# A decoder kernel on one core: the context first, row sums on 128 columns, late loads in two parts, and GpSimd in the rounding of the last causal steps

## The reference

```python
x = x + recurrent(ln(x), Wq1, Wq2, Wk1, Wk2, Wv, Wo, norm_w)  # q*scan(v), divided by its root mean square, @ Wo
x = x + experts(ln(x), token_ids, ctx, ctx, ctx)              # 4 experts, chosen by token id; ctx is the weight
x = x + ternary_linear(ln(x), weight, bias)
x = x + causal_attention(ln(x), w_project, w_out)             # 16 heads of 16
x = x + gqa_fp8(ln(x), cond=ctx, wq, wqx, wk, wv, w_kv_x, wproj)
#   xq = fp8(bf16(clip(ln_out / in_scale, -448, 448)))  for the four kinds q, qx, k, v
x = x + moe(ln(x), w_router, w_gate, w_up, w_down, shared...)
```

## Time and profile before

| | us |
|---|---|
| three timed runs | 924.49, 930.89, 932.22 |
| their median | 930.89 |
| the profiled execution | 927.09 |
| its span, first to last instruction | 924.3 |
| TensorE busy in the span | 857.9 (93%) |
| VectorE busy | 702.9 (76%) |
| ScalarE busy | 563.3 (61%) |
| GpSimd busy | 133.7 (14%) |
| mean granted clock of TensorE | 0.982 of full speed |

### The profile page before, as it was taken

The page is one execution under the profiler, slowest core; times in us unless marked ns, Lnnn a source line. Parts: engine busy times, 40 slices in busy tenths (PEclk is TensorE's granted clock), DMA queues, the critical chain, the costliest instruction groups (busy, mean ns, idle before and its releaser), DMA issues.

```text
span 924.3 us, 14815 instructions
## 1 busy us (share of the span) xinstructions
PE 857.9 (93%) x4742; PEld 637.8 (69%) x4742; DVE 702.9 (76%) x1573; ACT 563.3 (61%) x2045; POOL 133.7 (14%) x183
## 2 busy tenths in 40 slices
PE   5999999999887788999999999999999999899997
PEld 3656566656656666888787887878788787655554
DVE  3683553565777888888889898888988888897853
ACT  3542324575563966877778786877778687652311
POOL 3001020200001212212212121121212121100000
PEclk9999999899979998999999999999999999999999
DMA  7001000000100133242343343333332225420000
GB/s 235 1 0 57 1 0 1 1 2 1 54 6 23 58 79 81 70 106 67 78 109 100 72 123 72 86 86 81 89 87 75 69 69 165 109 71 21 1 23 23
DMA packets 63949, 56.72 MB, mean 61 GB/s; under 512 B 11073, under 2 KB 62850, under 8 KB 63874
## 3 DMA queue, kind: packets, MB, share of 16 engines
q1 hardware_dynamic: 63776, 55.76, 22.9%
q10 hardware_dynamic: 98, 0.03, 0.0%
HBM read 21.15 MB, written 1.05 MB: 24 GB/s over the span
## 4 chain that ended last, share of the span: by engine, by line
PE 66%; DVE 14%; ACT 7%; SPq 5%; issue 4%; DMA 2%; POOL 1%; DVEq 0%
PE ps L948 11%; PE ps L961 9%; PE ps L890 6%; SPq L589 5%; PE ps L976 4%; PE ps L1034 4%; PE ps L915 4%; PE ps L935 3%; PE ps L744 3%; PE ps L734 2%; PE ps L757 2%; ACT group_squares L1301 2%; PE ps L853 2%; PE ps L796 2%; PE ps L722 2%
## 5 line engine op out<-in xcount | busy, mean ns | idle before, releaser
L1359 ACT ACTIVATE group_probs<-ps,score_bias 128x256 f32<-128x256 f32 x256 | 117.4, 485 | 51.0 <-DVE score_bias L1789 51.0
L1789 DVE TENSOR_REDUCE score_bias<-ps 128x2 f32<-128x512 f32 x128 | 87.0, 690 | 40.9 <-PE ps L961 40.7
L961 PE MATMUL ps<-group_kT,group_qT 128*128 128x256 f32 x512 | 115.8, 379 | 0.6 <-ACT group_qT L1325 0.6
L961 PEld LDWEIGHTS ps<-group_kT,group_qT 128*128 128x128 f32 x512 | 97.1, 190 | 26.9 <-issue 8.4
L1301 ACT ACTIVATE group_squares<-ps 128x128 f32<-128x128 f32 x384 | 105.7, 347 | 9.4 <-PE ps L890 9.0
L1301 ACT ACTIVATION_READ_ACCUMULATOR group_squares<-ps 128x1 f32 x384 | 97.9, 280 | 0.0
L1347 ACT ACTIVATE group_cat_y<-ps,vec_inv 128x256 bf16<-128x256 f32 x128 | 53.9, 474 | 60.1 <-PE ps L948 57.1
L2133 POOL TENSOR_TENSOR head_rstd<-head_sum,minus_half 128x7 f32<-128x7 f32 (+1 forms) x64 | 86.8, 1356 | 5.3
L890 PE MATMUL ps<-group_w_hi,front_xq 128*128 128x256 f32 x256 | 74.1, 317 | 0.0
L2132 POOL TENSOR_SCALAR head_sum<-head_sum 128x7 f32<-128x7 f32 (+1 forms) x64 | 13.8, 215 | 415.3 <-ACT group_values_x L1316 415.2
L1800 DVE TENSOR_SCALAR group_probs<-group_probs,score_inv 128x256 f32<-128x256 f32 x256 | 72.7, 347 | 0.2
(11 more groups left out here) (294 smaller groups left out, 1947.2 us busy)
## 6 DMA issues: line engine op xcount, KB each, us to landing
second<-laid SPq DMA_DIRECT2D x256, 64.0 KB, 2.0
group_probsT<-front_quant SPq DMA_DIRECT2D x240, 64.0 KB, 2.0
group_raw_p<-in_L_xattn_wproj_dram SPq DMA_DIRECT2D x16, 256.0 KB, 3.3
group_raw_w<-in_L_xattn_wq_dram SPq DMA_DIRECT2D x8, 256.0 KB, 2.9
group_raw_w<-in_L_xattn_wqx_dram SPq DMA_DIRECT2D x8, 256.0 KB, 3.1
group_raw_w<-in_L_xattn_w_kv_x_dram SPq DMA_DIRECT2D x16, 128.0 KB, 3.2
x_all<-in_x_dram SPq DMA_DIRECT2D x2, 512.0 KB, 6.2
front_work<-in_ctx_dram SPq DMA_DIRECT2D x1, 1024.0 KB, 6.7
```

The lines of the kernel that those rows point to most:

```text
L961: last = pe.matmul(c.ps[:, bank, t * S:(t + 1) * S], c.qT[:, side, h, t * P:(t + 1) * P], c.kT[:, side, :], start=True, stop=True)
L1359: last = act.activation(c.probs[:, side, h, t, :], c.ps[:, fills.bank(name), t * S:(t + 1) * S], ACT.Exp, bias=c.score_bias[:, i:i + 1], a ...
L1789: v.tensor_reduce(c.score_bias[:, i:i + 2], c.ps[:, bank, :].rearrange("p (t n) -> p t n", n=S), AX.X, ALU.max, negate=True).then_inc(nega ...
```

## The change

1. ctx is loaded in four parts, right behind x of half 0 and each with a semaphore of its own; the token ids are loaded behind x of half 1. TensorE transposes ctx ahead of x, part by part, and ScalarE copies in that order.
2. `recur_out` multiplies the squares with 128 columns of ones in place of one; `ones` is 128 wide, and `take_sum` reads the first column of each 128.
3. `w_up` and `w_down` are issued in slot 30, behind that slot's moves, and have a semaphore on which `mix_basis(0, 0)` waits.
4. For half 0 and the kinds 0 to 2, VectorE stops after y + e and GpSimd subtracts e (`lower_kind`). VectorE's own subtraction of kind 3 waits for the three. The heads of step 13 are turned at the beginning of step 16, before `take_probs(15)`.

```diff
@@ -348,8 +348,8 @@
         if n >= 1 and n % 2:
             acc(h, n // 2)
 
+    take(*[("ctx", n) for n in range(NE)])
     take(("xT", "R", 0, 0), ("xT", "R", 0, 1))
-    take(*[("ctx", n) for n in range(NE)])
     take(("hid", 0, 0), ("hid", 0, 1))
     for n in range(NF):
         gates(0, n)
@@ -483,9 +483,8 @@
         wproj = a["L1_xattn_wproj"].rearrange("(o p) (s g n) -> o g p s n", p=P, s=2, g=G)
         LOADS, KV_LOADS, P_LOADS = 4, 2, 2
         late = [(c.w_router, a["L1_ffn_w_router"].rearrange("(k p) n -> p k n", p=P)),
-                (c.w_gate, a["L1_ffn_w_gate"].rearrange("(k p) n -> p k n", p=P)),
-                (c.w_up, a["L1_ffn_w_up"].rearrange("(k p) n -> p k n", p=P)),
-                (c.w_down, a["L1_ffn_w_down"])]
+                (c.w_gate, a["L1_ffn_w_gate"].rearrange("(k p) n -> p k n", p=P))]
+        late_up = [(c.w_up, a["L1_ffn_w_up"].rearrange("(k p) n -> p k n", p=P)), (c.w_down, a["L1_ffn_w_down"])]
         late_shared = [(c.w_sgate, a["L1_ffn_shared_w_gate"].rearrange("(k p) n -> p k n", p=P)),
                        (c.w_sup, a["L1_ffn_shared_w_up"].rearrange("(k p) n -> p k n", p=P)),
                        (c.w_sdown, a["L1_ffn_shared_w_down"].rearrange("(k p) n -> p k n", p=P))]
@@ -541,14 +540,15 @@
                     return a[w].rearrange("(k p) n -> p k n", p=P)
 
                 sp.dma_start(x[0], c.x_in[0]).then_inc(x_loaded[0], 16)
-                sp.dma_start(c.tok_rows[:], c.tok_in).then_inc(token_loaded, 16)
+                for n in range(NE):
+                    sp.dma_start(raw[:, n], a["ctx_2048"][n].rearrange("(r p) i -> p r i", p=P)).then_inc(ctx_loaded[n], 16)
                 sp.dma_start(c.w_q1, whole("L0_attn_Wq1")).then_inc(w1_loaded, 16)
                 sp.dma_start(c.w_k1, whole("L0_attn_Wk1")).then_inc(w1_loaded, 16)
-                sp.dma_start(raw[:, 0:4], a["ctx_2048"].rearrange("e (r p) i -> p e r i", p=P)).then_inc(ctx_loaded, 16)
                 sp.dma_start(c.w_q2, a["L0_attn_Wq2"]).then_inc(w2_loaded, 16)
                 sp.dma_start(c.w_k2, a["L0_attn_Wk2"]).then_inc(w2_loaded, 16)
                 sp.dma_start(c.w_v, whole("L0_attn_Wv")).then_inc(w2_loaded, 16)
                 sp.dma_start(x[1], c.x_in[1]).then_inc(x_loaded[1], 16)
+                sp.dma_start(c.tok_rows[:], c.tok_in).then_inc(token_loaded, 16)
                 sp.dma_start(raw_tern, a["L0_ffn_weight"].rearrange("(r p) i -> p r i", p=P)).then_inc(tern_loaded, 16)
                 sp.dma_start(raw[:, 5:8], a["L1_attn_w_project"].rearrange("(s r p) i -> p s r i", s=3, p=P)).then_inc(
                     proj_loaded, 16)
@@ -619,12 +619,16 @@
                         fills.wait_full(sp, ("proj", LATE_SLOT, 3))
                         for tile, src in late:
                             sp.dma_start(tile, src).then_inc(late_loaded, 16)
+                    if o.n == LATE_SLOT + 1:
+                        for tile, src in late_up:
+                            sp.dma_start(tile, src).then_inc(up_loaded, 16)
                 for moved in probs_moved:
                     sp.wait_ge(moved, (ITEMS // 2) * (16 * MOVES))
                 sp.wait_ge(raw_p_loaded, 16 * P_LOADS * G)
                 sp.wait_ge(raw_loaded, 16 * LOADS * G)
                 sp.wait_ge(raw_kv_loaded, 16 * KV_LOADS * (G // 2))
                 sp.wait_ge(late_loaded, 16 * len(late))
+                sp.wait_ge(up_loaded, 16 * len(late_up))
                 sp.wait_ge(shared_loaded, 16 * len(late_shared))
                 for h in range(2):
                     sp.wait_ge(result, HT * h + HT)
@@ -647,8 +651,8 @@
                         fills.wait_drained(pe, ("xT", stage, h, k))
 
                 def context():
-                    pe.wait_ge(ctx_loaded, 16)
                     for n in range(NE):
+                        pe.wait_ge(ctx_loaded[n], 16)
                         turn_square(("ctx", n), raw[:, n])
 
                 def turn_square(name, src):
@@ -675,9 +679,9 @@
                     turn_square(("square", "ternary"), tern[:, 0])
 
                 def recur_in(h):
-                    turn_tokens("R", h, xn[h], normed_count("R"))
                     if h == 0:
                         context()
+                    turn_tokens("R", h, xn[h], normed_count("R"))
                     turned("R", h)
                     pe.wait_ge(w1_loaded, 32)
                     for n, w in enumerate((c.w_q1, c.w_k1)):
@@ -710,7 +714,7 @@
                     bank = fills.claim(pe, ("sum", h))
                     for t in range(HT):
                         for f in range(NF):
-                            last = pe.matmul(c.ps[:, bank, t:t + 1], square[h][f][:, t * P:(t + 1) * P], c.ones[:, 0:1],
+                            last = pe.matmul(c.ps[:, bank, t * P:(t + 1) * P], square[h][f][:, t * P:(t + 1) * P], c.ones[:],
                                              start=f == 0, stop=f == NF - 1)
                     fills.filled(last, ("sum", h))
                     pe.wait_ge(out_ready[h], NF)
@@ -1026,6 +1030,8 @@
                             fills.filled(last, name)
 
                 def mix_basis(h, t):
+                    if h == 0 and t == 0:
+                        pe.wait_ge(up_loaded, 16 * len(late_up))
                     for i in range(4):
                         name = ("basis", h, t, i)
                         bank = fills.claim(pe, name)
@@ -1437,9 +1443,9 @@
                     act.dma_start(c.vec_rows[at:at + rows, :], src.rearrange("(r p) -> r p", p=P)).then_inc(vec_loaded, 16)
                 act.wait_ge(ident_ready, 1)
                 act.activation(c.small[:, 8:9], c.ident[:, 0:1], ACT.Sigmoid)
-                take_tokens("R", 0)
                 for n in range(NE):
                     take_square(("ctx", n), c.ctxT[:, n])
+                take_tokens("R", 0)
                 take_hidden(0)
                 for f in range(NF):
                     take_gates(0, f)
@@ -1645,7 +1651,7 @@
 
                 def take_sum(h):
                     bank = fills.wait_full(v, ("sum", h))
-                    fills.drain(v.tensor_copy(c.sums[:, h, :], c.ps[:, bank, 0:HT]), ("sum", h))
+                    fills.drain(v.tensor_copy(c.sums[:, h, :], c.ps[:, bank, :].rearrange("p (t n) -> p t n", n=P)[:, :, 0]), ("sum", h))
 
                 def recur_tail(h):
                     v.wait_ge(rms_root, h + 1)
@@ -1734,7 +1740,12 @@
                     y, e = y16[h][:, n % 2, :], e16[h][:, n % 2, :]
                     order.wait()
                     order.link(v.tensor_scalar(e, e, 2.0 ** -6, 24.0, ALU.max, ALU.mult))
+                    if h == 0 and n < 3:
+                        v.tensor_tensor(y, y, e, ALU.add).then_inc(lifted, 1)
+                        return
                     order.link(v.tensor_tensor(y, y, e, ALU.add))
+                    if h == 0:
+                        v.wait_ge(split_kind, n)
                     v.tensor_tensor(c.xq[:, h, KIND_ORDER[n], :, :], y.rearrange("p (k n) -> p k n", k=KD),
                                     e.rearrange("p (k n) -> p k n", k=KD), ALU.subtract).then_inc(split_kind, 1)
 
@@ -1992,6 +2003,8 @@
                 take_moments("T", 1, x[1])
                 for i in range(STEPS + 1):
                     if i == STEPS:
+                        turn_heads(i - 3)
+                        take_heads(i - 3)
                         take_probs(i - 1)
                     if i in QUANTISED and i > QUANT_STEP + 1:
                         clamp(0, QUANTISED[i])
@@ -2033,9 +2046,8 @@
                         normalise("C", 1, x[1], xn[1], normed[1])
                     for w in FIRST_STEPS.get(i, ()):
                         take_weight(("W", 0, w), w, 0)
-                for i in (STEPS - 3, STEPS - 1):
-                    turn_heads(i)
-                    take_heads(i)
+                turn_heads(STEPS - 1)
+                take_heads(STEPS - 1)
                 for o in SLOTS[:ITEMS + 1]:
                     visit(o)
                 last_turn, last_average, last_output = SLOTS[ITEMS + 1:]
@@ -2125,6 +2137,13 @@
                     pool.wait_ge(hidden_ready, NH * h + NH)
                     pool.memset(v_tok[h].rearrange("p e a n -> p (e a n)"), 1.0).then_inc(v_filled, 1)
 
+                def lower_kind(n):
+
+                    y, e = y16[0][:, n % 2, :], e16[0][:, n % 2, :]
+                    pool.wait_ge(lifted, n + 1)
+                    pool.tensor_tensor(c.xq[:, 0, KIND_ORDER[n], :, :], y.rearrange("p (k n) -> p k n", k=KD),
+                                       e.rearrange("p (k n) -> p k n", k=KD), ALU.subtract).then_inc(split_kind, 1)
+
                 def head_scale(o, t):
                     pool.wait_ge(proj_read, 4 * o.n + 2 * t + 2)
                     count = 7 if o.leads else 5
@@ -2152,6 +2171,8 @@
                 root_of("C", 1)
                 root_of("Q1", 0)
                 root_of("Q2", 0)
+                for n in range(3):
+                    lower_kind(n)
```

(8 more changed lines are left out.)

## The result

| us | before | changed |
|---|---|---|
| median of the first comparison (10 runs each) | 928.86 (922.98 to 932.22) | 918.24 (916.83 to 922.84) |
| ratio, 95% interval | | 0.9912 (0.9885 to 0.9939) |
| second comparison, in a later session (27 and 10 runs) | 928.28 | 918.32, ratio 0.9915 (0.9883 to 0.9947) |
| mean over all runs of the study (102 and 20) | 926.9 | 919.0 |
| profiled execution | 927.09 | 917.73 |

The changed kernel is faster by 0.9%: within the 1% that had most of the chance, but its median lies 1.3 us under the lower end of the range (919.5). The medians of before in these two comparisons are high draws: over 102 runs its median is 926.3. That takes some 2.5 us off the 10.6 between the first two medians. The gain is then about 8 us, where the sum had 3.5. So the forecast that the change stays within 1% held, with a sum that is less than half of what was measured.

The account below looks back on a forecast made before the run. TensorE was taken as the bound, with 66% of the chain. The terms 2.4 + 1.2 + 0.8 - 0.9 = 3.5 us came off 929.0, giving 925.5 us; own range 922 to 929, full range 919.5 to 933.

Parts of the forecast that it names:

- A: Kernel start: ctx loaded in four parts and transposed ahead of x; first projection 2.4 us sooner, ends 1.9 and 3.0.
- B: Row sums on 128 columns of ones: clock need not fall under the output projection; net 1.2 us, from -1.2 to 1.2.
- C: End of group stage: w_up and w_down issued behind the moves of slot 30; 0.8 us gained, ends 0 and 2.0.
- D: End of causal attention: three subtractions to GpSimd, heads turned a step sooner; VectorE held, so a cost of 0.9 us.
- rival 3: Kernel start: pauses between ctx loads leave the array slow, first projection takes 3.4 us more; 928.9 us, chance 0.15.
- the price of 0.25 us twice: Row sums: 32 records on 128 columns take 3.7 us against 3.46 on one column, +0.25 us in each half.
- once, since the second row sums show no fall: Output projection: the 1.7 us of clock fall behind one-column row sums counted for the first half only.
- The queue loses its two delays: SyncE's queue at slot 30: without the two weight loads the 16 moves take 10.17 us, not 10.97; 0.80 us gained.
- Rivals 1: Causal attention end: GpSimd holds only VectorE's two-input operations, masks run on; 2.8 us gained there, 921.8 us, chance 0.2.
- 2 (GpSimd at 3.5 us and more): Causal attention end: GpSimd's subtraction slower, at 4.2 us costing 6.7 us there; 931.3 us, chance 0.15.
- GpSimd get the port behind the clamp: Causal steps: VectorE starts its next clamp first, then GpSimd's 2.3 us subtraction holds the mask, first to 273.3 us.
- Faster by over 1% needs nothing held and a lucky clock: Whole kernel: gain above 9.3 us only if GpSimd holds no VectorE operation and the clock is lucky; chance 0.07.

Follow-up runs that it names:

- moved heads: Changed kernel with all subtractions back on VectorE and only the heads of step 13 turned a step sooner; median 919.17 us, ratio 0.9928 against before.

## Why the prediction was right, and where its sum was too small

| part | forecast | by the traces | by the times |
|---|---|---|---|
| A | 2.4 | 2.41 in the profiled pair, 2.17 of it at the row sums; 2.6 there on the mean | 1.7 alone |
| B | 1.2 | 1.69 in the profiled pair, 3.4 on the mean over executions | 4.9 alone, 3.5 taken out |
| C | 0.8 | 0.48, and 1.0 more by the clock | 2.4 alone, 0.6 taken out |
| D | -0.9 | -0.2 | -1.7 alone, -1.4 put on A to C |
| sum | 3.5 | 7.3 | 7.9 (926.9 to 919.0) |

- **A was right in place and size.** ctx transposes from 5.63 us, done at 9.28, x transposes at 9.47, projection at 11.96, forecast at about 12. The eight records of the projection took 3.67 us, full speed: rival 3 did not come about.
- **B is the term that was mis-sized.** The lengths were right to a tenth or so (3.57 us for 32 records on the chain, forecast 3.7; the first projection 6.92, forecast 7.0), but the price of 0.25 us twice was not: sums and projection together take 10.64 us in either form. The step that failed is "once, since the second row sums show no fall". It read one execution as the kernel. In three of six the second sums did let the clock fall, and in one of six the first fall was 3.35 us long in place of 1.69. B is worth 3.4 us on the mean, where the sum had 1.7 before the price and 1.2 behind it. The Trainium skill, TensorE: Matmul & The Clock Gate, Part 1, says that the chip judges activity over windows that do not start with the kernel, so the point of the change varies from run to run; the executions here agree (no fall, 1.69 or 3.35 us behind the same 32 instructions).
- **C failed in one step and gained in another.** "The queue loses its two delays": it lost one. The 16 moves take 10.48 to 10.64 us, forecast 10.2, so the load of `w_gate`, which stays in front, or what moves beside it, costs the other half; which of them was not tried. What the forecast did not have is the fall of the clock, seen behind waits of 2.10 to 2.21 us.
- **D was right in its mechanism, instruction by instruction**: GpSimd 2.24 us where 2.3 was taken, both masks and the head product held, the heads laid within 0.2 us of the old mean. Rivals 1 (two-input operations only: the masks would have run in 0.43 us) and 2 (GpSimd at 3.5 us and more) fall. The size against the profiled execution was off by 1.5 us (a gain of 0.6 where a cost of 0.9 stood). The working had GpSimd get the port behind the clamp, so that the first two holds ended 2.8 us behind the addition; GpSimd starts beside the clamp, and they end 2.3 us behind it (addition done at 262.27, subtraction at 264.59 us). That is 1.0 of the 1.5 us; the rest are tenths along the way. Against the mean over seven executions D costs 0.2 us. In both pairs with and without D the times say more (-1.7 and -1.4 us, clock loss higher by 2.7 and 2.5 us); each of these differences of time is within its uncertainty. The profiles do not show where D should cost clock: outside the row sums and the wait of slot 30 five with D lose 14.9 us of it on the mean, seven with neither D nor moved heads 14.3, and both groups spread over 11 to 19. It stays open.
- **The chances.** "Faster by over 1% needs nothing held and a lucky clock" gave the wrong reason: with all three held, the clock alone nearly did it, and that it stopped at 0.9% is luck as far as the prediction's working goes. The forecast's own range was also mis-added: A to C by their ends give 923.7 to 929.2 us with D at its middle, not 922 to 929. That the four executions of before spread over 8 us was read as noise to sit in the middle of. It was in large part a matter of half-clock stretches, and B, and as it seems C, took some of them away.

Sum by the traces 7.3 us (2.6 + 3.4 + 1.5 - 0.2), measured 7.9 with about 1.2 of uncertainty: nothing is left that needs another cause. The means of the traces rest on five to eight executions a place, so the agreement is closer than they can promise.

## What to carry to other kernels

Where one kernel's runs spread by a per cent and the mean clock of each run is known, hold the two against each other first: here 0.71 us per us of clock loss. A one-column matmul sequence, or a wait of 2 us, must then be priced by how often the clock falls behind it over several executions, not by one profile: 128 columns in place of one cost nothing with the clock up and took 3.4 us on the mean away. The work handed to GpSimd shortened this stretch (20.95 us against 21.79) only where VectorE had operations that read PSUM to do meanwhile; they were put there by hand.

## What the runs showed of the hardware

- GpSimd's subtraction, 128x1024, two bf16 inputs to fp32, took 2.12 to 2.24 us, no more than its fp32 addition: VectorE's factor of 1.77 between types on top of that addition, which would be 4.2 us, did not come. A VectorE mask or clamp of 1024 bf16 columns that starts under it is held until 0.28 us behind its end (2.23 and 1.98 us in place of 0.43), and so is the product of two SBUF tiles (1.53 in place of 0.42); row maxima, copies and head turns from PSUM (1.02, 0.68 and 0.71 us) and the reciprocal of 128x16 from SBUF (0.25 us) are not. The Trainium skill, Advanced Engine Details and Errata, VectorE Performance Modes, states the block for instructions that use both ports; the rows of masks, clamp and product agree, and show that it lasts as long as the GpSimd instruction.
- A fall of the clock costs in steps: 0, 1.69 or 3.33 to 3.35 us behind the row sums, 0 or 1.70 us behind the wait of slot 30, nothing between, in the 26 places looked at (12 one-column sums, 14 waits).
- Executions of one kernel differ by where the clock falls, while VectorE's and GpSimd's rows repeat to 0.01 or 0.03 us (the stretch with D: 22.70 to 22.73 us in five executions of four kernels).
